# Second attention of a fused transformer kernel: the order of score and value products, and of the inversion of the row sums

## What is computed

```python
def _L1_xattn_ref(queries, keys, values, ...):     # 16 heads of 64, 128 learned memory rows
    q = (queries @ wq_w + wq_b)                    # 512 queries
    k = concat(keys @ wk_w + wk_b, mk)             # 512 + 128 = 640 keys
    v = concat(values @ wv_w + wv_b, mv)
    attn = softmax(q @ k.T / sqrt(64))             # for each head
    return concat_heads(attn @ v) @ wo_w + wo_b
x = x + _L1_xattn_ref(layernorm(x), ctx, ctx, ...)
```

## Time and profile before

| | |
|---|---|
| median of 3 runs | 1547.67 us |
| lowest and highest | 1545.13, 1551.35 us |
| profiled execution | 1540.11 us, its span 1538.3 us |
| mean granted TensorE clock | 0.936 of full speed |
| second attention, from its first loop pair to the last product with values | about 724 to 1390 us of the span |
| TensorE busy over the span | 1377.1 us (90%) |

### The profile page before, as it was taken

The page is one execution under the profiler, slowest core; times in us unless marked ns, Lnnn a source line. Parts: engine busy times, 40 slices in busy tenths (PEclk is TensorE's granted clock), DMA queues, the critical chain, the costliest instruction groups (busy, mean ns, idle before and its releaser), DMA issues. The chain is left out here.

```text
span 1538.3 us, 19109 instructions
## 1 busy us (share of the span) xinstructions
PE 1377.1 (90%) x6106; PEld 733.4 (48%) x6106; DVE 876.9 (57%) x1738; ACT 477.4 (31%) x678; POOL 450.0 (29%) x262
## 2 busy tenths in 40 slices
PE   4889889989554999966999999999999999998997
PEld 2324333343352776642444455444544455435886
DVE  5656666555341222236576655756576665786677
ACT  1343434435111222211333332333233332341221
POOL 2000000000123000031454534445354543473443
PEclk8799999899756999986999999999999999999998
DMA  6410112101238988844556552655256552610001
GB/s 181 162 43 8 51 40 55 42 22 23 68 122 252 319 309 312 313 117 107 88 77 96 83 83 42 97 82 83 41 82 96 82 82 43 113 63 21 0 1 55
DMA packets 71273, 152.13 MB, mean 99 GB/s; under 512 B 17888, under 2 KB 28640, under 8 KB 64544
## 3 DMA queue, kind: packets, MB, share of 16 engines
q1 hardware_dynamic: 65392, 143.82, 41.2%
q0 software_dynamic: 2640, 7.21, 1.4%
q10 hardware_dynamic: 3168, 0.20, 0.1%
HBM read 75.49 MB, written 10.22 MB: 56 GB/s over the span
## 5 line engine op out<-in xcount | busy, mean ns | idle before, releaser
L1198 POOL TENSOR_TENSOR a_probs<-a_probs 128x1024 f32<-128x1024 f32 x128 | 304.9, 2382 | 379.2 <-PE a_p_mo L1868 378.7
L1270 ACT ACTIVATE a_probs<-a_p_s 128x1024 f32<-128x1024 f32 x160 | 163.8, 1024 | 340.7 <-PE a_p_s L1854 340.7
L468 DVE CUSTOM_DVE_ANT_0 a_scratch<-a_p_m,a_bias_q 128x512 bf16<-128x512 f32 x256 | 163.3, 687 | 97.3 <-PE a_p_m L639 97.2
L1502 DVE TENSOR_REDUCE a_max_ctx<-a_p_mo 128x1 f32<-128x512 f32 x256 | 161.5, 684 | 75.1 <-PE a_p_mo L1825 75.1
L362 ACT ACTIVATE a_probs<-a_p_s 128x1024 f32<-128x1024 f32 x128 | 129.1, 1024 | 113.6 <-PE a_p_s L677 112.3
L1868 PE MATMUL a_p_mo<-a_probs,a_v 128*64 128x512 f32 x512 | 139.0, 621 | 0.0
L1853 PE MATMUL a_p_s<-a_q_hh,a_k_hl 128*128 128x512 f32 x256 | 128.5, 502 | 0.0
L639 PE MATMUL a_p_m<-a_k_stack,a_q_stack 63*128 63x512 f32 x256 | 88.9, 543 | 24.3 <-DMA a_k_stack<-a_hi 22.1
L1525 DVE RECIPROCAL a_recip<-a_p_mo 128x512 f32<-128x512 f32 x32 | 107.4, 3355 | 5.0 <-PE a_p_mo L1877 4.9
L1854 PE MATMUL a_p_s<-a_q_lm,a_k_h 65*128 65x512 f32 x256 | 101.9, 398 | 0.0
L1246 ACT ACTIVATE a_o_norm<-a_p_mo,a_b 128x128 f32<-128x128 f32 x184 | 49.9, 382 | 151.9 <-PE a_p_mo L1730 151.9
(11 more groups left out here) (221 smaller groups left out, 2110.3 us busy)
## 6 DMA issues: line engine op xcount, KB each, us to landing
a_w<-in_L_w SPq DMA_DIRECT2D x46, 1024.0 KB, 6.6
a_q_hh<-a_hi SPq DMA_DIRECT2D x64, 256.0 KB, 5.1
a_k_hl<-a_hi SPq DMA_DIRECT2D x64, 128.0 KB, 6.1
a_k_hl<-a_lo SPq DMA_DIRECT2D x64, 128.0 KB, 6.5
a_k_h<-a_hi SPq DMA_DIRECT2D x32, 256.0 KB, 7.8
a_q_lm<-a_lo SPq DMA_DIRECT2D x32, 256.0 KB, 6.8
a_ctx_t<-in_ctx_t SPq DMA_DIRECT2D x8, 512.0 KB, 4.3
a_q_stack<-a_hi SPq DMA_DIRECT2D x64, 64.0 KB, 2.2
```

What stands on the lines that cost most here:

```text
L468: dve.tensor_tensor_reduce(scratch[:, fill.n % M_BANKS, :], m, bias_q[:, t, :], 1.0, -3.0e38, ALU.add, ALU.max, mx[:, g % 2, at:at + 1]).t ...
L1198: pool.tensor_tensor(probs[:, kt], probs[:, kt - 1], probs[:, kt], ALU.add)\
L1270: act.activation(probs[:, kt, :, :], p_s[:, (KT1 * p + kt) % 2, :, :], ACT.Exp).then_inc(exp_done.sem, 1)
L1502: dve.tensor_reduce(max_ctx[:, NT * head + t:NT * head + t + 1], m, AX, ALU.max)\
```

## The change

The scores of two key tiles are issued in a row, and the products with the values of two tiles in a row, behind the scores of the next two tiles. `total` is issued first in the last group, ahead of the last tile's scores and the last two maxima, and the VectorE inverts the sums at that place. The first `times_v` of a pair is still that of the last tile of the pair before. The output projection comes in two groups of two, the second value projection behind the products of the first two tiles. The number and shape of all instructions stay as they are. One wait is added: the score of the second tile of a sequence waits for the last exponential of the sequence before, which had been implied by the order.

```diff
-        STEPS = (("query", "score", "score", "turn", "key", "times_v"),
-                 ("out", "score", "score", "maximum", "maximum", "maximum", "times_v", "value"),
-                 ("out", "score", "score", "maximum", "maximum", "maximum", "times_v", "value"),
-                 ("out", "score", "score", "maximum", "maximum", "times_v", "rows"),
-                 ("out", "score", "maximum", "maximum", "total", "score", "times_v"))
+        SCORE, MAX3, OUT2 = ("score", "score"), ("maximum",) * 3, ("out", "out")
+        STEPS = (("query", *SCORE, *SCORE, "turn", "key", "times_v"),
+                 (*MAX3, *OUT2, "value", *SCORE, *SCORE, *MAX3, "times_v", "times_v", "maximum", "maximum"),
+                 ("value",),
+                 (*OUT2, "rows"),
+                 ("total", *SCORE, "maximum", "maximum", "times_v", "times_v"))
@@ scalar
-                                heads += 1
-                                if heads == 2:
-                                    exps(b, p, kt, total)
-                            elif what == "times_v" and kt == 0 and (p or behind):
-                                read_output(b, p - 1)
+                                n_score += 1
+                                if n_score % 2 == 0:
+                                    exps(b, p, n_score // 2 - 1, total)
+                            elif what == "times_v":
+                                if n_v == 0 and (p or behind):
+                                    read_output(b, p - 1)
+                                n_v += 1
@@ vector
-                            if what == "times_v" and kt == 4 and (p or behind):
-                                normalize(b, p - 1, *total)
-                            elif what == "total":
+                            if what == "total":
                                 m = fill.bank()
-                                total = m, fill.n, freed
+                                normalize(b, p - 1, m, fill.n, freed)
                             elif what == "out":
-                                add_output(b, fill, kt - 1, 1)
+                                add_output(b, fill, n_out, 1)
+                                n_out += 1
@@ tensor
-                if n >= 2 and i == 0:
+                if i == 0 and (n >= 2 or n == 1 and not (isinstance(b, int) and b == 0)):
                     exp_done.wait(pe, b, n - 1)
@@
-                                score(b, p, kt, head)
-                                head += 1
-                            elif what == "times_v" and kt:
-                                times_v(b, p, kt - 1)
-                            elif what == "times_v" and (p or behind):
-                                times_v(b, p - 1, KT1 - 1)
+                                score(b, p, n_score // 2, n_score % 2)
+                                n_score += 1
+                            elif what == "times_v":
+                                if n_v:
+                                    times_v(b, p, n_v - 1)
+                                elif p or behind:
+                                    times_v(b, p - 1, KT1 - 1)
+                                n_v += 1
@@
-                                project_out(b, banks, kt - 1)
+                                project_out(b, banks, n_out)
+                                n_out += 1
```

More of the change, by code:

```diff
@@ L1280, in turn @@
                     total = None
+                    n_score = n_v = 0
                     for kt in range(KT1):
-                        heads = 0
                         for what in steps(p, kt, ahead, behind):
@@ L1588, in turn @@
                 for p in range(PAIRS):
-                    i = half = 0
+                    i = half = n_out = 0
                     for kt in range(KT1):
@@ L1916, in turn @@
                 for p in range(PAIRS):
-                    i = half = 0
+                    i = half = n_score = n_v = n_out = 0
                     first = None
                     for kt in range(KT1):
-                        head = 0
                         for what in steps(p, kt, ahead, behind):
```

## The result

The changed kernel takes 1576.1 us (median of 4 runs, 1573.0 to 1578.6) where the kernel before took 1546.4 beside it (4 runs, 1542.0 to 1551.4): a ratio of 1.0177, with a 95% interval from 1.0142 to 1.0212. It is 1.8% slower; the forecast was 1543.2 us. The profiled execution took 1576.8 us, its span 1575.0.

The account below looks back on a forecast made before the run. TensorE's instruction queue was taken as the bound. Switches saved 21.8 us, less waits of 11.8, 1.0, 4.9 and 1.7, plus 0.3, 0.65, 0.6 and 0.8: 4.75, say 4.5, so 1547.7 becomes 1543.2 us (range 1532 to 1551).

Parts of the forecast that it names:

- What bounds the kernel: Second attention: a queue of TensorE instructions, busy 648 of 656 us; other engines matter only through the banks they free.
- Price of the switches, and what they save: TensorE shape switches: about 0.20 us to the full array, 0.14 to 64 columns; fewer of them save 21.8 us.
- rival (a): Each doubled value product pays 0.09 us at its seam, 6 us in all: about 1549 us; chance 0.12.
- Waits 1 and 2: TensorE waits for banks: third maximum 0.42 us in 28 pairs (11.8 us), value projection behind it 0.29 us (4.9 us).
- Rival (b): TensorE meets free banks; 16.7 us of bank waits stay away wholly or by half: 13 to 21 us faster; chance 0.14.
- Wait 3, the inversion: Query projection waits for total's bank: 0.12 us in 14 pairs, 1.7 us; at pair 5, about 2.1 us.
- Edits with one answer: Moved exponentials, GpSimd additions, `turn` and inversion cost nothing; additions end some 3 us before total, join 1.5 us before `turn`.
- "Inverted at once" is "worth nothing by itself": VectorE's early inversion of the sums gains nothing alone, since the inversion already had cover in three pairs per sequence and more.
- The last pairs: Last sequence, pairs 5 to 7: gains of 0.65 us from earlier scaling, 0.6 from a shorter wait, 0.8 from the clock.
- Rival (c), the clock: Waits of 0.4 to 0.7 us inside every pair drop TensorE's clock to 1.2 GHz: about 1557 us; chance 0.08.

## Why the prediction was wrong

*What bounds the kernel.* Right: TensorE's queue is the bound, and the loss is waits in it.

*Price of the switches, and what they save.* Right. With the hold away, by whichever means (tiny or half additions, product last, join as a reduction), plain odd pairs take 17.4 to 17.6 us, where about 17.5 was forecast, and even ones 21.2, as long as before. Doubled value products cost 1.87 us, as from 1071.20 to 1073.07 above, so rival (a) is out. The rule of the Trainium skill that stood beside it ("TensorE: Matmul & The Clock Gate", Part 3) doesn't hold for these loads, whose two products take 1.87 us together with no seam to be seen.

*Waits 1 and 2.* Right in place, and near in size. The list of waits shows only 16 at L1828, 0.26 us each. But the third maximum starts 0.62 to 0.75 us behind the second in all 28 pairs, and 0.33 us behind it with the key early, so that the wait is 0.29 to 0.42 us, where 0.42 was forecast. Moving the key took 0.4 to 0.5 us out of odd pairs (0.42 forecast), and moving the values 0.7 us out of even ones (0.29, and a switch of 0.34). Rival (b) is out.

*Wait 3, the inversion: the step that failed.* It priced the product at 0.75 us, and from this the prediction had the two reductions and their join "end 6.9 us after total's start, 1.5 us before `turn` needs them". Total began at 1073.50, the join ended at 1082.58: 9.1 us. Of the 2.2 us between, 1.27 are the held product and 0.87 the held join; the margin of 1.5 us was gone, and 0.7 us of waiting (0.96 - 0.24) came in its place, and 0.7 to 1.0 us in each of 24 pairs. The same hold made pair 5's wait 3.5 us instead of 2.1 (three times), since its query needs the banks of the reductions behind the product; without the additions it is 2.0 us, as forecast.

*Edits with one answer.* It weighed GpSimd's four additions only against `total`, whether they end in time, and the join only against `turn`. It didn't lay the two side by side. GpSimd and VectorE in the kernel before, in the pair of the earlier trace rows:

```profile
973.60 2.36 POOL L1198 TENSOR_TENSOR a_probs<-a_probs 128x1024 f32<-128x1024 f32 x1 [0.22 <-PE a_p_mo L1868]
977.54 2.35 POOL L1198 TENSOR_TENSOR a_probs<-a_probs 128x1024 f32<-128x1024 f32 x1 [1.59 <-PE a_p_mo L1868]
```
```profile
976.12 0.17 DVE L1511 TENSOR_TENSOR a_mx<-a_max_ctx,a_max_mem 128x8 f32<-128x8 f32 x1
```

The join ran 0.16 us after one addition had ended, and the product, at 979.70, came 0.2 us before the end of the other (979.89). Both cheap durations were owed to these places. The product was even held there already, by 0.06 us: 30 of the 32 products of the kernel before end 0.55 us after an addition, and 13 of these take 0.9 us. In the new order they come when the two products with values in a row have set two additions going back to back. The row that spoke of it was at hand: the product of the earlier trace rows took 1.76 us, beside the additions of the same group, and the prediction used that row only for TensorE's wait. So are the 10.24 us of six scalings there, beside additions; in the changed kernel, where VectorE was already in a row of such work when the addition began, the same six took 3.68 us and the addition 6.08:

```profile
1404.76 3.68 DVE L1565 TENSOR_TENSOR a_space<-a_space 128x512 f32<-128x512 f32 x6
```
```profile
1404.57 6.08 POOL L1200 TENSOR_TENSOR a_probs<-a_probs 128x1024 f32<-128x1024 f32 x1 [2.61 <-PE a_p_mo L1871]
```

*"Inverted at once" is "worth nothing by itself".* It cost 46 us by itself, and 34 us within the change (1576.1 against 1541.7). With the product behind the join it gains a little within the change (1535.5 against 1541.7, beside kernels before of 1549.7 and 1551.0): the intervals of the two ratios overlap, but the profiled executions agree with it, at 664.0 and 670.1 us from the first query projection to the last `total`.

*The last pairs.* Forecast 2 us better, measured 8.7 worse, by the same hold and by the clock behind it: the join's two longest waits, 2.5 us each, are here, and about 8 us of the loss by the estimate above are the 17 us more at the 1.2 GHz level. Gains elsewhere in these pairs weren't taken apart. Without additions the same stretch takes 66.7 us in place of 72.2, so GpSimd's additions count in it even before.

*Rival (c), the clock*, was named as what could make the kernel slower, by waits inside every pair. That part didn't come: the 24 waits at the turn were followed by no fall (1.00 from 1100 to 1143 us). But the clock has its share at the end, as above, so that the loss is waits and, in the last pairs, what the clock added to them; over the stage it was 0.98 against 0.99. It also cost 3.3 us a time in the experiment with the values between the scores and `total` late. No rival had a longer VectorE instruction in it: each put the loss into TensorE's own waits, with VectorE's durations fixed.

## What to carry to other kernels

A duration read from a profile holds for the neighbours it had there. When a step is moved, lay the timelines of VectorE and GpSimd side by side at its new place: for a VectorE instruction with two SBUF inputs, and for a `tensor_scalar` from SBUF to SBUF, an addition already running on GpSimd was a wait until about its end in every pair here. Put such instructions where no one waits for them, or, where it can be done, write them as reductions; and look at the largest duration of a line, not at its mean, for a sign of it. When an engine's busy time grows though it does the same work, look for what held it.

## What the runs showed of the hardware

- A join of 128 x 8 numbers took 0.17 us alone and 1.03 us (median), up to 2.17, beside an addition of 2.3 to 2.7 us on GpSimd; it ended 0.02 to 0.03 us after the addition each of 30 times. A product of 16 columns lasted 1.68 us (median), one of 512 columns 2.19 and ended 0.55 us after the addition each time.
- The hold depends on the form: a maximum of two SBUF tiles and a copy of one are held (1.03 and 1.04 us), a reduction over SBUF is not (0.17 us), nor are instructions that read PSUM (the memory's maxima at 0.64 us a piece). The trace of the kernel before has more of both kinds: the statistics of rows in SBUF (BATCH_NORM_STATS2) took 0.40 us beside an addition and without one, a `tensor_scalar` on 128x512 in SBUF 2.4 to 2.6 us beside one and 0.41 without.
- It goes both ways: GpSimd's addition took 2.64 us where VectorE's product ran into its start, 2.38 where not, and 6.08 us where it began during a row of VectorE's scalings.
- A wait of 0.95 us was followed by 6.8 us at the 1.2 GHz level (960.5 to 967.3), one of 0.68 us by as much in one execution and by none in another, and the two of 2.5 us in the changed kernel by 10.2 us each. From 1100 to 1143 us of the changed kernel, with waits of 0.65 and 0.67 us at the turn and two of 0.26 in it, the granted clock was 1.00.
